# Attention sums on VectorE: two groups taken in turn over the first eight key tiles of a query block

## Chip, cores and metric

The kernel runs on one core of one Trainium2 chip. The metric is the device time of one execution in microseconds (us). Times below come from the runs of the kernel before and from one profiled execution of it.

## What is computed

An attention layer, a residual and layernorm, a linear layer with sign weights, and again residual and layernorm. x is 4 x 2048 x 512 in fp32, with 16 heads of 32:

```
q, k, v = x @ Wq.T, x @ Wk.T, x @ Wv.T            # split into 16 heads of 32
attn    = softmax(q k^T / sqrt(32)) v
x       = layernorm(x + attn)
y       = clip((x @ sign(W).T) * scale + bias, -100, 100)
x       = layernorm(x + y)
```

The change is in the softmax's denominator: the sum over the keys of exp(energy), for each query and head.

## The kernel before, in words

Three stages follow each other: `project` (q, k and v for 16 blocks of 512 tokens), `attend`, and `normalise_and_ffn`. The change lies in `attend`.

`attend` works through 16 items (a batch entry and a group of 4 heads), 4 query blocks of 512 queries each, so 64 query blocks ("blocks" from here, counted from 0). In a block it goes over 16 key tiles of 128 keys. Each tile is two units (two heads each). The engines work like this:

- TensorE (PE), `steps`: in tile step kt it computes the scores of tile kt + 2 (`fast_scores`, L632, transposed: keys on partitions, queries along the free dimension; each unit waits until one of three PSUM slots is free), then the values product of tile kt (`values`, L661), and in tile steps 8 to 14 one of seven pieces of the denominators of the block before (`denominators`, L680), which sums over the partitions by a product with ones. Piece 0 waits for `a_merged`: all three merges of that block. PE takes these in program order.
- ScalarE (ACT), L769: one exponential of 128x1024 for each unit, from PSUM into `probs`, a ring of 8 tiles of 128x2048 fp32. It waits until the slot's old tile has been used by the values product (`a_pv`) and by VectorE (`a_sum`).
- VectorE (DVE), `item`: adds probability tiles. The 16 tiles form four groups. Group 0's sum is made in `total` (two buffers, by the block's parity), groups 1 to 3 in `partial` (one buffer each). Twelve adds a block: the first of a group adds two tiles (L818), and the others add a tile to the sum (L821). Tiles 0 to 3 are group 0, 4 to 7 group 1, 8 to 11 group 2, 12 to 15 group 3, and the adds come at tiles 1, 2, 3, 5, 6, 7, 9, 10, 11, 13, 14, 15. After tile 2's add it copies the block before's output from PSUM (`copy_out`, L797), and after tile 14's add the denominators (`copy_den`, L802). `a_sum` counts the tiles that are summed. An add that uses the sum of the add before waits for `a_sum`.
- GpSimd (POOL), `merge`, L601: for g = 1, 2, 3 it waits until `a_sum` says that the group's last tile is in, issues an accumulating DMA of 1 MB that adds `partial[g - 1]` to `total`, waits until it has landed (`a_merge`) and raises `a_merged`. So merges 1, 2 and 3 of a block run one after the other. In the last block merge 3 is left out, and PE takes both sums instead.
- SyncE (SP) issues the loads of the next item's rows and the stores. Most of the loads of k and v come in an item's fourth block, as tiles are finished; the rows of q come at the blocks' ends.

VectorE's order is written out by hand in `item`; the waits of the other engines are on counts of `a_sum`, `a_prob`, `a_pv`, `a_merged`, `a_den`, `a_out` and `a_dout`. `copy_den` of block b - 1 frees the PSUM bank that the values of block b + 1 write (`a_dout`).

Of the kernel before, what the change touches and what calls it, by code (L numbers as in the profile page):

```python
# [22 lines left out]
ALU = mybir.AluOpType  # L23
# [13 lines left out]
KT = S // P  # L37
# [12 lines left out]
NORM_SQ_MAX = 60000.0 ** 2 / BOUND_SLACK  # L50
GROUPS = 4
PER = KT // GROUPS
P_RING = 8
SLOTS = 3
LAG = 2
# [349 lines left out]
def attend(nc, ctx, dram, banks, ffn, first, early):  # L405
# [5 lines left out]
    def sb(name, shape, dt):  # L411
        return ctx.enter_context(nc.sbuf_tensor(name, shape, dt))

    def sem(name):
        return ctx.enter_context(nc.semaphore(name))
# [4 lines left out]
    k_exact = rows32[0:HD + 1, 1]  # L420
    probs = sb("probs", [P, P_RING, G, BLK], FP32)
    total = sb("total", [P, 2, G, BLK], FP32)
# [17 lines left out]
    a_sum = sem("a_sum")  # L440
# [31 lines left out]
    def out_bank(qb):  # L472

        return 2 * SLOTS + qb % 2
# [4 lines left out]
    def _(sp):  # L479
        def store(it, qb):  # L480

            cols = slice(qb * BLK, (qb + 1) * BLK)
            sp.wait_ge(a_out, it * QB + qb + 1)
            dst = dram["attn"].rearrange("n (g p) t -> (n g) p t", p=P)[bass.ds(it, 1), :, cols]
            sp.dma_start(dst.rearrange("o p t -> (o p) t"), out_sb[:, qb % 2, :]).then_inc(a_store[qb % 2], 16)
            sp.wait_ge(a_dout, it * QB + qb + 1 + 2)
            dst = dram["den"].rearrange("(i h) t -> i h t", h=G)[bass.ds(it, 1), :, cols]
            sp.dma_start(dst.rearrange("o h t -> (o h) t"), den_sb[0:P:HD, qb % 2, :]).then_inc(a_store[qb % 2], 16)
# [11 lines left out]
        with sp.If(needed > 0):  # L500
# [11 lines left out]
            def exact_block(it, n, g, qb, start):  # L512
# [8 lines left out]
                for c in range(QB):  # L521
# [6 lines left out]
                    if qb == 0 and c == 0 and not start:  # L528
                        sp.wait_ge(a_pv, st * KT + P_RING)
                        for vc in range(QB):  # L530
# [17 lines left out]
        with sp.Else():  # L548
# [4 lines left out]
            with sp.Fori(0, LAST) as it:  # L553
# [3 lines left out]
                for qb in range(QB):  # L557
                    st = it * QB + qb
                    if qb == QB - 1:
                        for c in range(QB):  # L560
# [3 lines left out]
                            if c > 0:  # L564
                                sp.wait_ge(a_pv, st * KT + TPB * c + P_RING)
                                load_v(sp, n_ahead, g_ahead, c - 1)
# [4 lines left out]
                    if 0 < qb < QB - 1:  # L571
                        store(it, qb - 1)
                sp.wait_ge(a_pv, (it * QB + QB) * KT + P_RING)
                load_v(sp, n_ahead, g_ahead, QB - 1)
# [8 lines left out]
    def _(pool):  # L583
# [11 lines left out]
        def merge(it, qb, groups):  # L595

            st = it * QB + qb
            for g in groups:
                pool.wait_ge(a_sum, st * KT + PER * (g + 1) + P_RING)
                pool.sem_inc(a_order, 1)  # L600
# [12 lines left out]
    def _(pe):  # L613
        pe.sem_inc(a_pv, P_RING)
        pe.sem_inc(a_den, 2 * len(DEN_TILES))
# [159 lines left out]
    @block.vector  # L775
    def _(dve):
        dve.sem_inc(a_sum, P_RING)
        dve.sem_inc(a_store[0], 32)
        dve.sem_inc(a_store[1], 32)
        needed = dve.value_load(flag[0:1, 0:1])  # L780
        with dve.If(needed > 0):
            dve.wait_ge(a_q[0], FIRST_Q)
            dve.wait_ge(a_k[0], FIRST_K)
            nc.vector.memset(k_exact[HD:HD + 1], 1.0).then_inc(m_ones, 1)
            with dve.Fori(0, N * H) as h:
                for t in range(KT):
                    dve.wait_ge(m_score, h * KT + t + 1)
                    nc.vector.reduce_max(maxima[:, t:t + 1], banks[:, 4 * (t % 2):4 * (t % 2) + 4, :]
                                         .rearrange("p b k -> p (b k)"), AX.X).then_inc(m_max, 1)
                dve.wait_ge(m_T, h + 1)  # L790
                dve.wait_ge(m_store, h * 16 + 16)
                nc.vector.tensor_scalar(max_neg[:], banks[0:KT, 0, 0:P], -1.0, None, ALU.mult).then_inc(m_neg, 1)

        def copy_out(st, parity):
            dve.wait_ge(a_pv, st * KT + KT + P_RING)
            dve.wait_ge(a_store[parity], (st - parity) * 16 + 32)
            nc.vector.tensor_copy(out_sb[:, parity, :], banks[:, out_bank(parity), :]).then_inc(a_out, 1)  # L797

        def copy_den(st, parity):
            dve.wait_ge(a_den, (st + 1 + 2) * len(DEN_TILES))  # L800
            dve.wait_ge(a_store[parity], (st - parity) * 16 + 32)
            nc.vector.tensor_copy(den_sb[:, parity, :], banks[:, out_bank(parity), :]).then_inc(a_dout, 1)  # L802

        def item(it, first):
            for qb in range(QB):
                st = it * QB + qb
                for kt in range(KT):
                    g, place = divmod(kt, PER)
                    if place == 0:
                        continue  # L810
                    into = total[:, qb % 2] if g == 0 else partial[:, g - 1]
                    dve.wait_ge(a_prob, st * UNITS + 2 * kt + 2 + SLOTS)
                    if place == 1:
                        if g == 0:
                            dve.wait_ge(a_den, (st + 1) * len(DEN_TILES))
                        else:
                            dve.wait_ge(a_merged, st * (GROUPS - 1) + g)
                        nc.vector.tensor_tensor(into, probs[:, (kt - 1) % P_RING], probs[:, kt % P_RING], ALU.add).then_inc(a_sum, 2)  # L818
                    else:
                        dve.wait_ge(a_sum, st * KT + kt + P_RING)  # L820
                        nc.vector.tensor_tensor(into, into, probs[:, kt % P_RING], ALU.add).then_inc(a_sum, 1)  # L821
                    if kt == OUT_AFTER and not (first and qb == 0):
                        copy_out(st - 1, (qb - 1) % 2)
                    if kt == DEN_AFTER and not (first and qb == 0):
                        copy_den(st - 1, (qb - 1) % 2)

        for it in range(ITEMS):
            item(it, it == 0)
        copy_out(ITEMS * QB - 1, 1)
        copy_den(ITEMS * QB - 1, 1)  # L830
# [292 lines left out]
class Early:  # L1123
# [26 lines left out]
    def load_v(self, sp, n, g, c):  # L1150
        src = self.v_src[bass.ds(n, 1), bass.ds(g, 1), c].rearrange("o u p t d -> p (o u t) d")
        sp.dma_start(self.v_keys[:, c * TPB:(c + 1) * TPB, :], src).then_inc(self.a_v[c], 16)
# [63 lines left out]
```

## Time and profile before

| what | us |
|---|---|
| runs | 2725.27, 2724.6, 2723.04 |
| median | 2724.6 |
| profiled execution: span from its first to its last instruction | 2721.4 |
| busy in the span: PE, VectorE, ScalarE, GpSimd | 2686.9, 2308.4, 2261.1, 341.1 |
| attention stage, first exponential's start to last one's end | 549.9 to 2427.7 |

The profile gives the profiled execution's span alone; what lies around it isn't shown, and the median of the runs stands 3.2 us above the span. PE's ends are modelled, so its busy time says little about what it could still take. The line numbers are those of the kernel before. A merge's busy time on POOL (0.86 us) is that of issuing it; "to landing" is from its start to the end of its transfer.

### The profile page before, as it was taken

The page shows a single profiled execution, that of the slowest core. Times are in us where ns is not written, and L with a number is a line of the kernel's source. Part 1 is how long each engine was busy: PE and PEld are TensorE (multiplying, and loading weights), DVE is VectorE, ACT ScalarE, POOL GpSimd, SP SyncE. Part 2 cuts the span into 40 slices and gives each one's busy share as a digit, 9 for nine tenths or more (in the row PEclk, how much of TensorE's full clock was granted, in tenths as well). Part 3 has the DMA queues.
Part 4 walks back from the last instruction along what each step waited for, and adds up shares of the span by engine and source line. Part 5 has one row for each costly group of instructions (what it writes and reads, how often), then busy time and mean ns, then how long its engine had stood idle before and what let it go on. Part 6 is the DMA issues. An engine that isn't in the chain of part 4 may idle for free.

```text
span 2721.4 us, 76294 instructions
## 1 busy us (share of the span) xinstructions
PE 2686.9 (99%) x32088; PEld 1351.0 (50%) x32088; DVE 2308.4 (85%) x1983; ACT 2261.1 (83%) x2726; POOL 341.1 (13%) x342
## 2 busy tenths in 40 slices
PE   9999999999999999999999999999999999979998
PEld 8888888733333333333333333333333333337887
DVE  7444444389999999999999999999999999978998
ACT  5333333399999999999999999999999999965665
POOL 1000000000000000010000000000000000005665
PEclk9999999999999999999999999999999999989999
DMA  6555555557686777768677686867768677655553
GB/s 227 191 194 193 188 186 186 197 132 169 132 176 140 155 157 158 162 126 184 138 153 165 142 172 135 167 147 157 168 131 172 141 159 158 150 145 177 189 189 136
DMA packets 216706, 445.22 MB, mean 164 GB/s; under 512 B 15570, under 2 KB 130258, under 8 KB 189780
## 3 DMA queue, kind: packets, MB, share of 16 engines
q0 software_dynamic: 27504, 200.29, 37.4%
q1 hardware_dynamic: 179108, 222.61, 26.2%
q10 hardware_dynamic: 9792, 17.83, 1.7%
q8 instruction: 246, 4.03, 0.6%
q14 instruction: 56, 0.46, 0.1%
HBM read 122.43 MB, written 117.96 MB: 88 GB/s over the span
## 4 chain that ended last, share of the span: by engine, by line
ACT 48%; PE 31%; issue 16%; DMA 3%; DVE 2%; SPq 0%; DVEq 0%; POOL 0%; ACTq 0%; POOLq 0%
ACT probs L769 48%; PE banks L226 19%; PE banks L1007 7%; DMA total<-partial 2%; PE banks L632 1%; PE banks L996 1%; PE banks L661 1%; PE banks L989 1%; PE banks L1003 1%; DVE partial L818 1%; DVE total L821 0%; DVE partial L821 0%; PE banks L248 0%; PE banks L990 0%; PE banks L254 0%
## 5 line engine op out<-in xcount | busy, mean ns | idle before, releaser
L769 ACT ACTIVATE probs<-banks 128x1024 f32<-128x1024 f32 x2048 | 1877.7, 1457 | 3.9 <-PE banks L632 3.9
L632 PE MATMUL banks<-score_rows 97*32 97x512 f16 x16384 | 1117.4, 380 | 4.5 <-issue 4.0
L661 PE MATMUL banks<-probs,v_keys 128*32 128x512 f32 x8192 | 1060.5, 592 | 0.1
L821 DVE TENSOR_TENSOR partial<-partial,probs 128x2048 f32<-128x2048 f32 x384 | 879.4, 2290 | 33.4
L632 PEld LDWEIGHTS banks<-score_rows 97*32 97x32 f16 x16384 | 361.3, 95 | 708.2 <-ACT probs L769 484.3
L818 DVE TENSOR_TENSOR partial<-probs 128x2048 f32<-128x2048 f32 x192 | 439.6, 2290 | 23.6 <-ACT probs L769 16.7
L601 POOL DMA_DIRECT2D total<-partial x191 | 164.7, 862 | 1713.7 <-DMA total<-partial 703.3
L661 PEld LDWEIGHTS banks<-probs,v_keys 128*32 128x32 f32 x8192 | 249.0, 111 | 209.9 <-ACT probs L769 0.2
L821 DVE TENSOR_TENSOR total<-total,probs 128x2048 f32<-128x2048 f32 x128 | 292.6, 2286 | 6.8
L354 DVE TENSOR_TENSOR qk_lo<-banks,qk_hi 128x512 f16<-128x512 f32 x128 | 88.3, 690 | 241.6 <-ACT qk_hi L309 241.6
L680 PEld LDWEIGHTS banks<-total,ones 128*32 128x32 f32 x3584 | 105.6, 109 | 280.7 <-issue 265.1
L309 ACT ACTIVATE qk_hi<-banks 128x512 f16<-128x512 f32 x128 | 76.0, 595 | 184.6 <-PE banks L226 184.6
L226 PE MATMUL banks<-xT_hi,w_hi 128*128 128x512 f32 x512 | 197.3, 389 | 0.0
L226 PE MATMUL banks<-xT_lo,w_hi 128*128 128x512 f32 x512 | 197.2, 389 | 0.0
L226 PE MATMUL banks<-xT_hi,w_lo 128*128 128x512 f32 x512 | 197.2, 389 | 0.0
L818 DVE TENSOR_TENSOR total<-probs 128x2048 f32<-128x2048 f32 x64 | 146.2, 2284 | 7.3 <-ACT probs L769 7.3
L313 ACT ACTIVATE v_out<-banks 128x512 f32<-128x512 f32 x64 | 38.2, 597 | 123.9 <-PE banks L226 123.8
L680 PE MATMUL banks<-total,ones 128*32 128x72 f32 (+1 forms) x3584 | 134.7, 227 | 4.6 <-POOLq L603 4.5
L1021 ACT ACTIVATE std<-mean_var,eps 128x1 f32<-128x1 f32 x128 | 31.8, 289 | 98.0 <-DVE mean_var L1075 97.8
L226 PEld LDWEIGHTS banks<-xT_lo,w_hi 128*128 128x128 f32 x512 | 96.1, 188 | 20.0
L226 PEld LDWEIGHTS banks<-xT_hi,w_lo 128*128 128x128 f32 x512 | 96.1, 188 | 19.9
L226 PEld LDWEIGHTS banks<-xT_hi,w_hi 128*128 128x128 f32 x512 | 96.0, 188 | 19.9
(95 smaller groups left out, 2117.5 us busy)
## 6 DMA issues: line engine op xcount, KB each, us to landing
total<-partial POOLq DMA_DIRECT2D x191, 1024.0 KB, 8.3
scratch_q_raw<-qk_raw SPq DMA_DIRECT2D x16, 1024.0 KB, 5.7
scratch_k_raw<-qk_raw SPq DMA_DIRECT2D x16, 1024.0 KB, 5.7
scratch_v<-v_out SPq DMA_DIRECT2D x16, 1024.0 KB, 5.1
score_rows<-scratch_q_hi SPq DMA_DIRECT2D x128, 128.0 KB, 4.6
score_rows<-scratch_k_hi SPq DMA_DIRECT2D x128, 128.0 KB, 3.5
v_keys<-scratch_v SPq DMA_DIRECT2D x64, 256.0 KB, 5.8
scratch_attn<-wf_scaled SPq DMA_DIRECT2D x64, 256.0 KB
```

The costliest lines, as they stand in the source:

```text
L226: last = nc.tensor.matmul(bank(j), *parts[i], start=(c == 0 and i == 0), stop=(c == DC - 1 and i == 2))
L309: nc.scalar.activation(qk_hi[:, j, :], bank(j), ACT.Copy).then_inc(s_hi, 1)
L313: nc.scalar.activation(v_out[:, j - NQK, :], bank(j), ACT.Copy).then_inc(s_hi, 1)
L354: nc.vector.tensor_tensor(qk_lo[:, j, :], bank(j), qk_hi[:, j, :], ALU.subtract).then_inc(s_lo, 1)
L601: pool.dma_start(total[:, qb % 2], partial[:, g - 1], accum_op=ALU.add).then_inc(a_merge, 16)
L632: last = nc.tensor.matmul(scores_of(phase, unit)[part, i, :], k_rows[:, h, keys], q_rows[:, h, qb * BLK:(qb + 1) * BLK], start=True, stop= ...
L661: last = nc.tensor.matmul(banks[rows, out_bank(qb), :], v_keys[:, kt, rows], probs[:, kt % P_RING, h, :], start=(kt == 0), stop=(kt == KT ...
L680: last = nc.tensor.matmul(banks[rows, out_bank(qb), cols], ones[:], part[:, h, cols], start=(part is parts[0]), stop=(part is parts[-1]))
L769: nc.scalar.activation(probs[:, kt % P_RING, heads, :], scores_of(it % SLOTS, qb * UNITS + u), ACT.Exp, scale=SCALE / GAIN ** 2).then_inc( ...
L818: nc.vector.tensor_tensor(into, probs[:, (kt - 1) % P_RING], probs[:, kt % P_RING], ALU.add).then_inc(a_sum, 2)
L821: nc.vector.tensor_tensor(into, into, probs[:, kt % P_RING], ALU.add).then_inc(a_sum, 1)
L1007: last = nc.tensor.matmul(ffn_bank(s), part[:, s % 4, cols], w[:, c, :], start=False, stop=(c == DC - 1 and w is wf_lo))
```

## The change

VectorE's groups are no longer four consecutive tiles each: over tiles 0 to 7 they alternate, so group 0 has tiles 0, 2, 4 and 6, and group 1 has 1, 3, 5 and 7. Groups 2 and 3 stay 8 to 11 and 12 to 15. The adds come at tiles 2, 3, 4, 5, 6, 7, 9, 10, 11, 13, 14, 15. `PREVIOUS` is the tile of the same group before a tile. `TAKEN` says how many tiles, counted from 0 without a hole, are in a sum after a tile's step; `a_sum` is raised by its steps. An add to a sum waits for the add of its own group's previous tile, which in tiles 4 to 7 isn't the add just before. The merges, their conditions (`a_sum` at 8, 12 and 16 tiles) and everything else stay.

```diff
 GROUPS = 4
 PER = KT // GROUPS
+GROUP_OF = (0, 1) * PER + (2,) * PER + (3,) * PER
+PREVIOUS = tuple(max((e for e in range(kt) if GROUP_OF[e] == GROUP_OF[kt]), default=None) for kt in range(KT))
+
+
+def taken_after(kt):
+
+    used = {e for k in range(kt + 1) if PREVIOUS[k] is not None for e in (PREVIOUS[k], k)}
+    return next(e for e in range(KT + 1) if e not in used)
+
+
+TAKEN = tuple(taken_after(kt) for kt in range(KT))
...
                 for kt in range(KT):
-                    g, place = divmod(kt, PER)
-                    if place == 0:
+                    g, before = GROUP_OF[kt], PREVIOUS[kt]
+                    if before is None:
                         continue
                     into = total[:, qb % 2] if g == 0 else partial[:, g - 1]
                     dve.wait_ge(a_prob, st * UNITS + 2 * kt + 2 + SLOTS)
-                    if place == 1:
+                    if PREVIOUS[before] is None:
                         if g == 0:
                             dve.wait_ge(a_den, (st + 1) * len(DEN_TILES))
                         else:
                             dve.wait_ge(a_merged, st * (GROUPS - 1) + g)
-                        nc.vector.tensor_tensor(into, probs[:, (kt - 1) % P_RING], probs[:, kt % P_RING], ALU.add).then_inc(a_sum, 2)
+                        nc.vector.tensor_tensor(into, probs[:, before % P_RING], probs[:, kt % P_RING],
+                                                ALU.add).then_inc(a_sum, TAKEN[kt] - TAKEN[kt - 1])
                     else:
-                        dve.wait_ge(a_sum, st * KT + kt + P_RING)
-                        nc.vector.tensor_tensor(into, into, probs[:, kt % P_RING], ALU.add).then_inc(a_sum, 1)
+                        dve.wait_ge(a_sum, st * KT + TAKEN[before] + P_RING)
+                        nc.vector.tensor_tensor(into, into, probs[:, kt % P_RING], ALU.add).then_inc(a_sum, TAKEN[kt] - TAKEN[kt - 1])
```

## Rows read from the trace of the kernel before

**Rows 1.** The page: the costliest group of instructions (busy, mean of one, idle)

```profile
L769 ACT ACTIVATE probs<-banks 128x1024 f32<-128x1024 f32 x2048 | 1877.7, 1457 | 3.9 <-PE banks L632 3.9
```

**Rows 2.** Attention stage: busy us of PE, PEld, DVE, ACT, POOL; clock, DMA share, GB/s

```profile
549.90:2427.70 1877.80, 1876.67 (x28088) 688.60 (x28080) 1809.18 (x892) 1877.69 (x2048) 164.72 (x191) 1.00 0.72 152
```

**Rows 3.** The chain of waits in block 3: start, us, what

```profile
654.23 2.30 DVE partial L821
...
657.09 10.06 DMA total<-partial
...
667.87 10.76 DMA total<-partial
...
679.35 7.28 DMA total<-partial
...
686.73 0.34 PE banks L680 x8
```

**Rows 4.** The chain of waits at the end of the attention stage

```profile
2417.23 7.85 DMA total<-partial
...
2425.74 6.98 DMA total<-partial
```

**Rows 5.** VectorE in order of time, blocks 49 (end) and 50: start, us, instruction

```profile
2018.65 2.28 DVE L821 TENSOR_TENSOR partial<-partial,probs 128x2048 f32<-128x2048 f32 x1
2020.85 2.28 DVE L818 TENSOR_TENSOR total<-probs 128x2048 f32<-128x2048 f32 x1
2023.24 2.29 DVE L821 TENSOR_TENSOR total<-total,probs 128x2048 f32<-128x2048 f32 x1
2025.45 0.68 DVE L797 COPY wf_scaled<-banks 128x512 f32<-128x512 f32 x1
2026.05 2.28 DVE L821 TENSOR_TENSOR total<-total,probs 128x2048 f32<-128x2048 f32 x1
2028.25 2.28 DVE L818 TENSOR_TENSOR partial<-probs 128x2048 f32<-128x2048 f32 x1
2030.63 4.69 DVE L821 TENSOR_TENSOR partial<-partial,probs 128x2048 f32<-128x2048 f32 x2
...
2037.84 4.69 DVE L821 TENSOR_TENSOR partial<-partial,probs 128x2048 f32<-128x2048 f32 x2
2042.78 2.29 DVE L818 TENSOR_TENSOR partial<-probs 128x2048 f32<-128x2048 f32 x1 [0.25 <-ACT probs L769]
```

**Rows 6.** Timelines: first exponentials of blocks 50 and 4, PE in block 50

```profile
2016.52 1.43 ACT L769 ACTIVATE probs<-banks 128x1024 f32<-128x1024 f32 x1
667.03 1.43 ACT L769 ACTIVATE probs<-banks 128x1024 f32<-128x1024 f32 x1
2020.31 1.03 PE L661 MATMUL banks<-probs,v_keys 128*32 128x512 f32 x8
2035.80 0.31 PE L680 MATMUL banks<-total,ones 128*32 128x80 f32 x8
```

**Rows 7.** L769 alone, in block 50, then in block 4: duration ns min/median/max

```profile
L769 ACT ACTIVATE probs<-banks x33: 1388/1480/1618, 2015.6 to 2044.9; 128x1024 f32<-128x1024 f32 x33
L769 ACT ACTIVATE probs<-banks x33: 1017/1247/1442, 666.1 to 695.9; 128x1024 f32<-128x1024 f32 x33
```

**Rows 8.** L601's landings, and totals of waits (us, times, longest us)

```profile
DMA to landing us min/median/max: 6.9/8.3/11.1
...
POOL total L601 <- DMA total<-partial: 703.3, 86, 10.3
PEld banks L680 <- POOLq L603: 15.1, 17, 4.9
```

**Rows 9.** Columns of rows 2, block 51, whose first exponential starts at 2045.85

```profile
2045.85:2049.85 4.00, 4.00 (x68) 1.58 (x64) 4.00 (x3) 4.00 (x6) 0.00 (x0) 1.00 0.99 184
2060.00:2063.00 3.00, 3.00 (x48) 1.03 (x44) 2.90 (x2) 3.00 (x5) 0.00 (x0) 1.00 0.61 170
2063.00:2066.00 3.00, 3.00 (x56) 1.08 (x51) 2.88 (x2) 3.00 (x5) 0.77 (x1) 1.00 0.21 60
```

## The prediction

> **What bounds the kernel now.** I read the busy totals first. In the attention stage ScalarE's exponentials (L769) fill 1877.7 us of 1877.8 [rows 1, 2], 0.917 us each, so one query block (32 exponentials) takes 29.33 us and ScalarE has nothing to win: 2048 x 0.9167 is 1877.3, so 0.4 us at most is idle. VectorE is 1809.2 us busy in the same stretch [rows 2] and sits idle until ScalarE delivers (the add of tile 13, 2042.78) [rows 5]. A faster VectorE is therefore worth nothing by itself, and the question is whom VectorE's adds serve, and when.
>
> The chain of waits answers it. Through block 3 of 64 (counted from 0) it leaves ScalarE and runs: VectorE's adds up to tile 7's, then merge 1, merge 2 and merge 3 one after the other, then the first denominator matmul (L680) of the next block [rows 3]. It does so again at the end of the stage: merges 1 and 2 of the last block, released like that, hold the end [rows 4]. POOL issues merge 1 only when the add of tile 7 has ended (654.23 + 2.30 = 656.53, issue at 657.09), and each next merge 0.7 us after the last one landed [rows 3]; a merge takes 6.9 to 11.1 us, median 8.3 [rows 8]. Merge 3 must have landed when PE reaches the denominators in tile step 8 of the next block. I count times within a block from the start of its first exponential: 2016.52 for block 50, 667.03 for block 4. In block 50, undisturbed, the first denominator matmul starts at 2035.80, so at 19.28; in block 4 it starts at 686.73, 19.70, 0.10 after the landing at 686.63, 19.60 [rows 3, 6]. So the deadline for a landing is about 19.15. Behind it there is a cushion: exponentials start before the one ahead has ended. In block 50 they last at least 1.388 us, in block 4 the shortest lasts 1.017 us [rows 7]; 0.38 us of PE's lateness is swallowed that way, and a landing later than 19.53 costs time one for one.
>
> I tabulated all 63 landings of merge 3 (block 3's merge is the one in rows 3) against the first exponential of the block that needs them: 12.4 to 19.6, median 16.8. Block 4's and block 40's (19.60, 19.56) just exceed 19.53; the kernel today loses about 0.1 us to it.
>
> **The change, part by part.** The number of adds stays 12 a block, with the same operands in size, and the counts given to a_sum still sum to 16.
> (a) The first add moves from tile 1 to tile 2. In block 50 tile 13's add started when its tile was ready, at 26.26 [rows 5]; tile 2 is ready 11 x 1.833 earlier, at 6.09. The last add of the block before ends well ahead of that (see c). So the add starts at 6.09, where tile 1's started at 4.33 (2020.85).
> (b) The adds after it. An add that reads the result of the one just before starts 2.40 us after it (2037.84, 2.29 and so on; 2028.25 to 2030.63 is 2.38); one that doesn't starts 2.20 us after (2026.05 to 2028.25) [rows 5]. A copy sits 2.21 us after its add and the next add 0.60 after the copy. Now tiles 2 and 3, 3 and 4, up to 7 alternate: four steps of 2.20. Tile 3 starts at 6.09 + 2.21 + 0.60 = 8.90, tile 7 at 8.90 + 4 x 2.20 = 17.70. Before it was 2030.63 + 2.40 - 2016.52 = 16.51. **Tile 7's add comes 1.2 us later**, although three gaps of 0.19 us are saved: before, it had one more add behind it already.
> (c) The rest: tile 9 at 19.90, 10 at 22.3, 11 at 24.7 (+1.0), 13 at 26.9 (+0.6), 14 at 29.3, the denominator copy at 31.5, tile 15 at 32.1 (+0.6), free again at 34.3, which is 5.0 into the next block. VectorE then waits 1.1 us for tile 2 and the lag doesn't grow.
> (d) What waits for these. Probability slots: tile 0 is released after tile 2's add (8.4) and needed for tile 8, after 14.6; tile 15 after 34.4 - 29.3 = 5.1 and needed after 12.8: no cost. The denominator copy ends near 32.2, 2.9 into the next block; PE's first values there start at 3.79 (2020.31) [rows 6]: 0.9 us of cover is left of 1.6. The partial sum of group 1 is overwritten from 8.9 on, and the merge that reads it has landed by 1 us into the block. No queue gets another DMA; POOL's three waits a block are the same.
> (e) Merges 1, 2, 3. Merge 1 starts 1.2 later; merge 2 and 3 were held by the landing before them (86 of 191 issues by the profile [rows 8]; tile 11's and 15's adds end at 27.0 and 34.4, ahead of the new 29.7 and 39.4). So **merge 3 lands 1.2 us later**. This is the only thing that I price above nothing in the loop.
>
> **The sum.** With 1.2 added, a landing that was later than 18.33 loses. Seventeen are: 19.60, 18.93, 19.05, 18.56, 19.05, 18.62, 18.73, 18.43, 19.39, 18.56, 19.08, 19.27, 19.56, 19.11, 19.44, 19.04, 18.74; the excesses sum to 11.6 us. A replay block by block, with today's merge durations, in which a delay of one block leaves the next that much room, the cushion refills by 0.35 us a block and merge 1 waits for the later of the add and the last merge, gives 10.1. Most of the seventeen are merges of every fourth block (3, 7, 11, ...), in which the next item's rows are loaded: in block 51 the DMA share is 0.61 from 14.2 to 17.2 and 0.21 from there to 20.2, where merge 1 itself (issued at 19.4) has hardly begun [rows 9]. A merge 1 that starts 1.2 later passes the end of this traffic; between none and 0.3 us off these merges I take 0.2, and the replay gives 7.9. At the end merges 1 and 2 of the last block are on the chain [rows 4]: + 1.2. Today's own loss goes off: - 0.1. Together + 9.0 on an execution with a span of 2721.4. The median of the runs stands 3.2 above this span; I carry that over: 2724.6 + 9.0 = 2733.6 us.
>
> The replay is steep. With a shift of 0.4, 0.8, 1.0, 1.2, 1.4 us it gives 1.5, 5.0, 7.4, 10.1, 13.1 us; with every merge 3% longer 25, 3% shorter 1.
>
> **Rivals.**
> 1. The merges give it back (about no change). A merge's duration isn't fixed by its size: 6.9 to 11.1 us [rows 8], and DMA is 0.72 busy in this stage [rows 2]. If a chain that starts 1.2 us later meets less of the loads, its three merges together get shorter. The mechanism decides at 0.5 us off the chain of some 25: what is left of the shift then costs 4.5 us in the loop, with the end's 1.2 just 0.2%. With 0.8 off it is 1.5 + 0.4, so 2726.5. For it: the traffic in rows 9, and the latest landings of today that crowd at 19.0 to 19.1. Against it: merge 2 and 3 run across the start of the next block's loads (share 0.99 there [rows 9]) before and after. 0.22.
> 2. No gap is saved. If an add after an independent one also took 2.40, tile 7's add would start at 8.90 + 4 x 2.40 = 18.50, 2.0 later than today; the replay gives 22.8, the end 2.0: 2749. Against it stand the pairs of tiles 3 and 5 and of 15 and 1, at 2.20 in each block [rows 5]. 0.05.
> The Trainium skill, VectorE: DVE Perf Modes, The DRAIN you can't avoid, says this: every VectorE operation is followed by a pipeline flush, and eight chained copies took the same time with a semaphore after each as with one at the end, "the semaphore costs nothing extra here". By that rule alternating groups saves nothing; this case's trace disagrees, with 2.40 against 2.20 us from start to start.
> 3. Faster. ScalarE's idle 0.4 us is all that the loop could return, less than the 5.4 us (0.2%) that a measurement of this kernel can tell from no change; only a chain at the end that got shorter by several us could do it, and I see none. 0.02.
>
> **Chances and range.** Forecast with the loss as described: 0.71; rivals 0.22, 0.05, 0.02. So faster 0.02, same 0.22, slower 0.76. The range goes down to the case of the merges that give most of it back (2726.5) and up to merges about 1.5% longer than today on the late blocks (2746).
>
> **What would show it.** Tile 7's add starts near 17.7 in a block and the idle time of VectorE moves ahead of tile 2's add; consecutive adds of tiles 3 to 7 stand 2.20 apart. Merge 1 is issued at 20.6 instead of 19.4; merge 3's median landing is near 18.0. PE's waits for POOL at L680 grow from 15.1 us in all [rows 8], the chain of waits runs through the merges in some 15 blocks instead of two or three, and the attention stage grows by some 8 us while the stages before and after it keep their length. I would be wrong if merge 1 started no later, if the landings didn't follow it, or if a late landing had no echo in ScalarE's ends.

## The result: 0.22% slower, and the profile after

The changed kernel takes 2730.61 us (median of 10 runs, 2726.33 to 2734.31), the kernel before 2724.57 us (10 runs, 2722.43 to 2726.13). The ratio is 1.0022, 95% interval 1.0013 to 1.0031: 6.0 us, with the interval reaching from 3.5 to 8.4. The forecast was 2733.6 in a range of 2726.5 to 2746. Medians and ratios, here and below, leave out four executions in the slow state, of 4600 to 15800 us (three of the kernel before, one of the late start alone).

The profiled execution took 2733.11 us, with a span of 2731.3. It is one of the slower ones of its kernel, so the differences of the two profiles (9.9 us of span) overstate the median's. A second profile of each kernel is among the experiments below.

The attention stage, in the columns of rows 2 (PE, PEld, DVE, ACT, POOL, clock, DMA share, GB/s), answers to [rows 2]:

```profile
550.30:2438.60 1888.30, 1875.72 (x28091) 697.12 (x28080) 1786.66 (x892) 1880.06 (x2048) 164.57 (x191) 1.00 0.71 151
```

It lasts 1888.3 us where it lasted 1877.8: 10.5 longer, and this is where all the time went. VectorE is busy for 22 us less, though its work is the same: neighbouring adds that don't wait for each other overlap by 0.08 us, the view counts that once, and there are four more such pairs in a block (4 x 0.08 x 64 = 20 us, an estimate that leaves 2 us of the 22 unexplained). Fewer busy microseconds on an engine didn't make a faster kernel.

VectorE in block 50, whose first exponential starts at 2025.98, answers to [rows 5] (start, us, instruction, idle before it):

```profile
2028.65 2.28 DVE L833 TENSOR_TENSOR partial<-partial,probs 128x2048 f32<-128x2048 f32 x1
2031.98 2.29 DVE L829 TENSOR_TENSOR total<-probs 128x2048 f32<-128x2048 f32 x1 [1.04 <-ACT probs L780]
2034.18 0.68 DVE L808 COPY wf_scaled<-banks 128x512 f32<-128x512 f32 x1
2034.79 2.28 DVE L829 TENSOR_TENSOR partial<-probs 128x2048 f32<-128x2048 f32 x1
2036.98 2.28 DVE L833 TENSOR_TENSOR total<-total,probs 128x2048 f32<-128x2048 f32 x1
2039.19 2.28 DVE L833 TENSOR_TENSOR partial<-partial,probs 128x2048 f32<-128x2048 f32 x1
2041.39 2.28 DVE L833 TENSOR_TENSOR total<-total,probs 128x2048 f32<-128x2048 f32 x1
2043.59 2.28 DVE L833 TENSOR_TENSOR partial<-partial,probs 128x2048 f32<-128x2048 f32 x1
```

The idle 1.04 us ahead of tile 2's add is new. From tile 3 on the adds stand 2.20 apart. Tile 7's add starts at 2043.59, which is 17.61 in this block (median of the blocks 17.66), where it was 16.51. POOL issues merge 1 at 2046.54, 20.56 in the block; the median over the blocks is 20.52 after 19.39.

The chain of waits through block 39 into block 40, whose first exponential starts at 1730.41 (start, us, what):

```profile
1721.56 9.23 DMA total<-partial
...
1731.51 10.78 DMA total<-partial
...
1743.01 9.11 DMA total<-partial
...
1752.21 0.35 PE banks L691 x8
```

Merge 3 lands at 1752.12, 21.71 in the block. PE in order of time at that place:

```profile
1748.80 1.03 PE L672 MATMUL banks<-probs,v_keys 128*32 128x512 f32 x8
1752.21 0.35 PE L691 MATMUL banks<-total,ones 128*32 128x80 f32 x8 [2.38 <-POOLq L614]
1752.37 1.05 PE L643 MATMUL banks<-score_rows 97*32 97x512 f16 x16
```

PE stands for 2.38 us ahead of the first denominator piece, and the scores queued behind it come that much later. ScalarE's exponentials after it show that no cushion is left, since their shortest is what an exponential takes with nothing queued (duration ns, min/median/max, to compare with [rows 7]):

```profile
L780 ACT ACTIVATE probs<-banks x4: 1014/1020/1027, 1753.0 to 1755.8; 128x1024 f32<-128x1024 f32 x4
```

The waits in all (us, times, longest), to compare with 15.1 us in [rows 8]:

```profile
PEld banks L691 <- POOLq L614: 34.7, 24, 5.1
...
PE banks L691 <- POOLq L614: 16.7, 14, 4.2
...
ACT probs L780 <- PE banks L643: 12.1, 12, 4.3
```

The last row is ScalarE idle. In the kernel before it was idle once, 3.9 us, at the stage's start. Here the 4.3 us are that start, and eleven idle times inside the stage are new, 7.9 us together. In the page's shares of the chain that ended last, the merges ("DMA total<-partial") hold 13% of the span, where they held 2%.

### The profile page after: what moved, and what is told of

It is laid out like the page before. It is cut to its first block, busy times and chain, and to the rows that moved or that the text cites. A ratio compares the mean times of both kernels' runs of the same rounds, so it can differ in the third digit from the quotient of the medians.

```text
span 2731.3 us, 76294 instructions
## 1 busy us (share of the span) xinstructions
PE 2684.6 (98%) x32088; PEld 1358.4 (50%) x32088; DVE 2286.5 (84%) x1983; ACT 2263.3 (83%) x2726; POOL 340.9 (12%) x342
## 4 chain that ended last, share of the span: by engine, by line
ACT 31%; PE 21%; DMA 13%; issue 12%; DVE 1%; POOLq 0%; POOL 0%; SPq 0%; DVEq 0%; ACTq 0%
ACT probs L780 31%; DMA total<-partial 13%; PE banks L1019 6%; PE banks L643 6%; PE banks L672 6%; PE banks L1008 1%; PE banks L1001 1%; DVE partial L833 1%; PE banks L691 1%; PE banks L1015 1%; DVE partial L829 0%; PE banks L1002 0%; ACT y L1037 0%; DMA den_in<-scratch_den 0%; DVE stats L1082 0%
## 5 line engine op out<-in xcount | busy, mean ns | idle before, releaser
L780 ACT ACTIVATE probs<-banks 128x1024 f32<-128x1024 f32 x2048 | 1880.1, 1394 | 12.4 <-PE banks L643 12.1
L643 PEld LDWEIGHTS banks<-score_rows 97*32 97x32 f16 x16384 | 367.8, 95 | 700.1 <-ACT probs L780 469.4
L237 PEld LDWEIGHTS banks<-xT_hi,w_lo 128*128 128x128 f32 x512 | 96.1, 188 | 19.9
```

The lines of the kernel that those rows point to most:

```text
L237: last = nc.tensor.matmul(bank(j), *parts[i], start=(c == 0 and i == 0), stop=(c == DC - 1 and i == 2))
L643: last = nc.tensor.matmul(scores_of(phase, unit)[part, i, :], k_rows[:, h, keys], q_rows[:, h, qb * BLK:(qb + 1) * BLK], start=True, stop= ...
L780: nc.scalar.activation(probs[:, kt % P_RING, heads, :], scores_of(it % SLOTS, qb * UNITS + u), ACT.Exp, scale=SCALE / GAIN ** 2).then_inc( ...
```

## The experiments

Two numbers stand for each profile, both tabulated block by block as the prediction did for the kernel before: the **excess**, the sum of what merge 3's landings exceed 19.53 us by, and the **loss**, the sum of what the blocks from 1 on last beyond 29.33 us, from the end of one block's last exponential to the next (with 29.33 taken as 32 x 0.9167 = 29.333). The theory was that merge 1 starts later, merge 3 therefore lands later, and what is late beyond the cushion is lost. The rivals were that VectorE's own later adds and its later denominator copy cost the time, that the alternation itself does, or that the runs differ for another reason.

**A later merge with VectorE untouched.** In the kernel before, a clear of 128x1100 on GpSimd between merge 1's wait and its issue:

```diff
             for g in groups:
                 pool.wait_ge(a_sum, st * KT + PER * (g + 1) + P_RING)
+                if g == 1:
+                    pool.wait_ge(m_spin, st + 1)
+                    pool.sem_inc(a_order, 1)
+                    nc.gpsimd.memset(spin[:], 0.0).then_inc(m_spin, 1)
+                    pool.wait_ge(m_spin, st + 2)
```

(The lines that make `spin` and its semaphore are left out, here and in the next run.)

> The kernel before with one clear of 128x1100 on GpSimd put between merge 1's wait for VectorE and merge 1's issue in every block; VectorE's order is untouched. Theory (the cost of the change is merge 1 starting late, so that merge 3 misses TensorE's first denominator piece): merge 1 is issued about 1.1 to 1.3 us later (estimate from the 0.53 us of a 128x512 clear on GpSimd), merge 3's landings move as much, some 13 to 15 blocks lose time, + 5 to + 12 us against the kernel before. Rival (the cost comes through VectorE's own later adds and later denominator copy): no change, within 2 us, since VectorE does nothing later.

Measured: 2733.74 us (5 runs) against 2723.91 (27 runs), ratio 1.0036 (1.0023 to 1.005), + 9.8 us. The clear takes 1.02 us; merge 1 is issued at 20.58 (median), the waits at the denominators grow as in the changed kernel:

```profile
PEld banks L688 <- POOLq L611: 37.1, 29, 5.3
PE banks L688 <- POOLq L611: 15.4, 14, 4.4
ACT probs L777 <- PE banks L640: 11.5, 9, 4.3
```

and the stage lasts 1886.8 us with VectorE's adds where they were (tile 7's at 16.51):

```profile
550.00:2436.80 1886.80, 1875.52 (x28088) 696.83 (x28080) 1809.44 (x892) 1879.52 (x2048) 229.55 (x255) 1.00 0.71 151
```

So a merge that starts 1.2 us later is enough for the whole cost. The rival of VectorE's later adds isn't needed. By the medians this run is even 3 us slower than the changed kernel, though its excess and loss lie between those of the changed kernel's two profiles (the table below). Its last stage is 1.2 us longer, with more of it at the lower clock (the last section), and the rest isn't explained; the two intervals, 6.3 to 13.6 us and 3.5 to 8.4, overlap.

**The same clear where it should be hidden**, ahead of merge 1's wait:

```diff
             for g in groups:
+                if g == 1:
+                    pool.wait_ge(m_spin, st + 1)
+                    pool.sem_inc(a_order, 1)
+                    nc.gpsimd.memset(spin[:], 0.0).then_inc(m_spin, 1)
+                    pool.wait_ge(m_spin, st + 2)
+                    pool.sem_inc(a_order, 1)
                 pool.wait_ge(a_sum, st * KT + PER * (g + 1) + P_RING)
```

> The same clear, but ahead of merge 1's wait for VectorE, where GpSimd is idle. Theory: no change, within 2 us of the kernel before, landings as before. A rival for the run with the clear behind the wait (the clear itself disturbs VectorE or the transfers): as slow as that run.

Measured: 2726.54 us (11 runs), ratio 1.0011 (1.0002 to 1.002), + 2.6 us: more than expected, and the step that I had overlooked is visible. The clear is hidden only while POOL is idle there. Where merge 3 of the block before lands late, the clear starts after it: after landings at 19.16 and 19.32 merge 1 is issued at 21.54 and 21.69 instead of 19.4 to 20.5. In most blocks merge 1 goes at 19.40 as before. The excess is 3.5 us, the loss 3.5, in four blocks. It is a weak dose of the same mechanism, not a free control; it does show that the clear by itself does no harm in the other 60 blocks. That the loss again equals the excess, to 0.1 us, speaks for the chain too, since here the clear moved only some of the merges.

**The deadline moved.** The denominators in six pieces from tile step 9 on, in the changed kernel and in the kernel before:

```diff
-DEN_TILES = tuple(range(8, 15))
-DEN_EDGES = (0, 80, 152, 224, 296, 368, 440, BLK)
+DEN_TILES = tuple(range(9, 15))
+DEN_EDGES = (0, 88, 172, 256, 340, 424, BLK)
```

> The changed kernel with the denominators in six pieces at tile steps 9 to 14 instead of seven at 8 to 14, so that TensorE wants merge 3's landing 1.85 us later. VectorE's adds are as in the changed kernel. Theory: no landing of merge 3 is late any more; the loss in the attention stage goes to below 1 us, the time returns to within 2 us of the kernel before. Rival (VectorE's later adds of tiles 13 to 15 and its later denominator copy cost the time): it stays 4 to 8 us slower than before.

> The kernel before with the same six pieces at tile steps 9 to 14. Theory: few of its landings are late, so at most 1 us is gained, and the difference between this run and the changed kernel with six pieces is within 1.5 us: that is what the change costs when the deadline is moved. Should the larger pieces cost TensorE time by themselves, both six-piece kernels show it.

Measured: the changed kernel with it 2724.49 us (11 runs), ratio to the kernel before 1.0002 (0.9993 to 1.0011); the kernel before with it 2722.41 (11 runs), ratio 0.9994 (0.9985 to 1.0003), 1.5 us less where at most 1 was expected, and not told from no change. The stage of the changed kernel with it, in which VectorE is as late as without it (tile 7's add at 17.58, tile 15's at 31.98):

```profile
550.20:2428.00 1877.80, 1877.80 (x27588) 678.72 (x27577) 1785.52 (x892) 1877.54 (x2048) 164.51 (x191) 1.00 0.71 152
```

Four of its landings are still later than 19.53 (excess 3.1), and the loss is 0.02: lateness costs nothing once TensorE asks for the sum a tile later. Between the two six-piece kernels 2.1 us are left, a little more than the 1.5 expected. Of these 0.2 is the stage; the last merge of the stage lands 5.60 us after the last exponential in the one and 4.21 in the other, which is the cost at the stage's end (+ 1.4). Some of the 2.1 may be TensorE's clock: the mean granted clock over the whole execution was 0.992 in eight of the eleven runs of the one and in one of the eleven of the other, and the last section shows that such runs are the longer ones.

**The late start alone.** The kernel before with its groups and gaps; only tile 1's add waits for tile 2:

```diff
-                    dve.wait_ge(a_prob, st * UNITS + 2 * kt + 2 + SLOTS)
+                    late = 1 if kt == 1 else 0
+                    dve.wait_ge(a_prob, st * UNITS + 2 * (kt + late) + 2 + SLOTS)
```

> The kernel before, its groups and all its gaps kept, with the first add of a block waiting for tile 2 instead of tile 1: the late start of the change alone. Theory: tile 7's add starts at 6.09 + 2.40 + 2.21 + 0.60 + 2.20 + 2.40 + 2.40 = 18.3, 1.8 us later than before and 0.6 later than in the changed kernel; the replay gives about 19 us in the loop: + 12 to + 22 us against the kernel before, clearly slower than the changed kernel. Rival (the alternation costs the time, the late start doesn't): within 2 us of the kernel before.

Measured: 2735.66 us (5 runs) against 2723.73 (21 runs), ratio 1.0044 (1.0031 to 1.0057), + 11.9 us. Tile 7's add starts at 18.26, merge 1 goes at 21.16. It lies just under what was expected: the replay's 19 us was too much, the profile has a loss of 12.5, with 16 landings beyond 19.53. So of the two halves of the change the late start costs 12 us, and the alternation gives 6 of them back.

**The same with the deadline moved**, the edit of the six pieces on top:

> The late first add of the kernel with all gaps kept (it was 12.2 us slower than before), with the six denominator pieces at tile steps 9 to 14. Its landings of merge 3 are the latest of all. Theory: at most one or two blocks still lose time; the loss in the loop falls from 12.5 us to under 1.5, the time to + 1 to + 3.5 us against the kernel before, with 1.2 of it at the stage's end. Rival (VectorE's own lateness costs): it stays more than 8 us slower.

Measured: 2724.95 us (11 runs), ratio 1.0004 (0.9995 to 1.0013). Fourteen landings lie beyond 19.53 (excess 8.7) and the loss is 0.02. What was 11.9 us is 0.9, just under the 1 to 3.5 that were expected.

**The alternation without the late start.** In the changed kernel's code:

```diff
-GROUP_OF = (0, 1) * PER + (2,) * PER + (3,) * PER
+GROUP_OF = (0, 0, 0, 0, 1, 1, 0, 1) + (2,) * PER + (3,) * PER
```

> Groups of tiles 0, 1, 2, 3, 6 and of 4, 5, 7: the adds come at tiles 1, 2, 3, 5, 6, 7 as in the kernel before, and the adds of tiles 5, 6 and 7 alternate. So two gaps go without the late start. Theory: tile 7's add starts 0.4 us earlier than before, merge 3 lands 0.4 earlier; - 1 to + 0.5 us against the kernel before, since little was lost there. Rival (alternating groups is itself what costs): slower than before by over 2 us.

Measured: 2722.86 us (11 runs), ratio 0.9995 (0.9986 to 1.0004), - 0.9 us and not told from no change. Tile 7's add starts at 16.14 (0.38 earlier), merge 1 at 19.01. The adds of tiles 5, 6 and 7 stand 2.20 apart. Alternating costs nothing.

**And with the copy of the output behind tile 7's add** (`OUT_AFTER = 7` on top of it):

> The same groups, and the copy of the output moved from behind tile 2's add to behind tile 7's: merge 1's wait ends 0.8 us earlier than in the kernel before, the copy ends at about 18.2 in the block, ahead of the 19.15 at which TensorE's first denominator piece wants it. Theory: - 2 to 0 us against the kernel before, of which up to 0.8 at the end of the stage. Should the copy come too late for TensorE, it shows as waits for VectorE at the denominators.

Measured: 2724.18 us (11 runs), ratio 1.0002 (0.9993 to 1.0011). Merge 1 goes at 18.88, only 0.13 earlier than without it and 0.51 earlier than in the kernel before, where 0.8 was expected: with the copy gone, tile 3's add needs the 2.40 again and tile 5's waits for its tile. No landing is late, so there was nothing left to win.

**The two edits for the better together**, tiles 5 to 7 alternating after an early start, and the six pieces:

> The groups 0, 1, 2, 3, 6 and 4, 5, 7 together with the six denominator pieces at tile steps 9 to 14: merge 1 starts 0.4 us earlier than before and the deadline is 1.85 us later. Theory: the attention stage is at the pace of the exponentials (1877.3 to 1877.8 us) in every execution, merges at the stage's end come 0.4 us earlier; - 2.5 to - 0.5 us against the kernel before, and a narrower spread upwards. Rival (the kernel before loses nothing by its landings): no change.

Measured: 2723.71 us (11 runs) against 2724.03, ratio 0.9998 (0.9989 to 1.0007): no gain that can be told from none, where 0.5 to 2.5 us were expected. No landing is later than 18.9, and the runs reach from 2721.66 to 2724.24. The stage took 1878.8 us, outside the 1877.3 to 1877.8 that were expected for every execution: its blocks from 1 on lose nothing, but block 0, ahead of which there is no merge, took 30.75 us, after 29.62 in the kernel before. None of these versions is measurably faster than the kernel before, which fits a stage that already runs at the pace of its exponentials.

**Second profiles of both kernels.**

> The changed kernel once more, for a second profile. Theory: the spread of its runs (2726.3 to 2734.3) is that of merge 3's landings: the loss in the attention stage differs from the first profile's 10.0 us by about as much as the whole time does, and equals the sum of what its landings exceed 19.53 by. Rival: the stage is as long as in the first profile and the difference lies in the other stages.

> The kernel before once more, for a second profile. Theory: its landings of merge 3 lie on the near side of 19.53 in all but a few blocks again, the attention stage lasts 1877.5 to 1880 us.

Measured: 2730.8 us and 2723.73 us, spans 2729.0 and 2721.9. The stages, changed kernel first:

```profile
550.00:2436.50 1886.50, 1874.85 (x28093) 696.93 (x28082) 1786.88 (x892) 1879.30 (x2048) 164.48 (x191) 1.00 0.71 151
```
```profile
549.80:2427.50 1877.70, 1877.17 (x28092) 690.53 (x28080) 1809.68 (x892) 1877.58 (x2048) 164.49 (x191) 1.00 0.72 152
```

The changed kernel's span is 2.3 us shorter than in its first profile, 1.8 of it in the stage (loss 8.0 after 10.0). The theory of the spread is that the merges' durations differ between executions and a late landing is now paid for, while in the kernel before most of that variation falls short of the deadline. These two profiles fit it, and so does the changed kernel with the deadline moved: its eleven runs lie within 2.2 us, where the ten without that spread over 8.

All profiles together, in us:

| kernel | tile 7's add | merge 1 issued | excess | loss |
|---|---|---|---|---|
| before, two profiles | 16.52, 16.52 | 19.39, 19.43 | 0.1, 0.2 | 0.2, 0.2 |
| changed, two profiles | 17.66, 17.66 | 20.52, 20.52 | 10.2, 7.9 | 10.0, 8.0 |
| before, clear behind the wait | 16.51 | 20.58 | 8.7 | 8.6 |
| before, clear ahead of the wait | 16.53 | 19.40 | 3.5 | 3.5 |
| before, late start | 18.26 | 21.16 | 12.1 | 12.5 |
| before's start, tiles 5 to 7 alternating | 16.14 | 19.01 | 0.1 | 0.0 |
| the same, copy of the output behind tile 7 | 16.01 | 18.88 | 0.0 | 0.0 |
| before, six pieces | 16.46 | 19.34 | 0.0 | 0.0 |
| changed, six pieces | 17.58 | 20.44 | 3.1 | 0.0 |
| late start, six pieces | 18.22 | 21.09 | 8.7 | 0.0 |
| tiles 5 to 7 alternating, six pieces | 16.08 | 18.95 | 0.0 | 0.0 |

In every kernel of the table with the deadline at step 8 the loss equals the excess within 0.4 us. The two are read from different places, the landings of the transfers and the ends of the exponentials, and that is the theory's strongest support. The times in the second and third column are medians over the blocks.

## Why the prediction was right, point by point

- **What bounds the kernel**: as said. The exponentials' pace sets the stage wherever no landing is late (1877.4 to 1878.0 us, and 1878.8 once, through block 0), and the saved gaps on VectorE gain nothing there. The edge of 19.53 was rounded: the rows give 19.28 - 0.10 + 0.37 = 19.55, a difference that changes none of the readings.
- **(a), (b), (c), VectorE's times**: tile 2's add at 6.05 (forecast 6.09), tile 7's at 17.66 (17.70), tile 15's at 32.05 (32.1). The saved gap is 0.19 us, four in a row at 2.20. Rival 2, that nothing is saved, is out.
- **(d), what was priced at nothing**: the runs with the deadline moved leave VectorE as late as in the changed kernel, and the stage loses nothing; no other wait took over.
- **(e), the merges**: merge 1 starts 1.13 us later (forecast 1.2). Merge 3's median landing moved less, from 16.8 to 17.4, where 18.0 was forecast: the shift shrank in the three easy blocks of four and stayed nearly whole in the fourth (from 18.9 to 20.0 in the mean, in the second pair of profiles from 19.0 to 19.9), and those are the ones that count.
- **The size of the loss**: 7.9 us forecast in the loop, 10.0 and 8.0 in the two profiles. One term had the wrong reason: I took 0.2 us off merge 1 in every fourth block for the loads that it would miss, and there it took 9.3 us in the mean after 8.9, in both pairs of profiles, while merge 3 took 0.3 to 0.4 less. The three merges of those blocks together changed by + 0.1 us in the first pair and - 0.1 in the second, so the term was nearly nothing. Without it the replay said 10.1. It said 19 for the late start, which lost 12.5, so its agreement at 1.2 us is partly luck: it holds the merges' durations fixed, and they aren't.
- **The cost at the stage's end** was put at 1.2 us and wasn't paid in the profiles: the last landing came 5.21 and 5.23 us after the last exponential, after 5.03 and 5.38 before, because the last block's merge 1 was shorter (6.9 us in both, before 7.9 and 8.1). In the six-piece pair it was 1.4. The term is real on average at most, and hidden in the merges' spread.
- **The last stage** was assumed unchanged. It was 1.3 to 1.8 us shorter, see below. This and the point above come to some 3 us, as much as 2733.6 was too high; the sizes are those of two profiles, so that the sum fits is in part chance.
- **Rival 1**, that the merges give it back, had 0.22. It holds in part: the chains of three blocks in four did get shorter (their three merges by 0.2 us in the mean), and the late ones didn't by more than 0.1.

## What to carry to other kernels

On an engine that isn't the bound, count not how busy it is but when its result for someone else is ready: follow the chain from there to the engine that is, find the deadline and the cushion, and tabulate the slack over all rounds, since the mean slack (here over 2 us) says nothing about the few rounds that pay. A reordering that removes gaps but starts later moves the result by the late start less the gaps, and both have to be worked out up to the result that someone waits for. Where durations vary between executions, moving the deadline by one step can do more than shaving the chain: here it took back 5.4 of 6.0 us and 11.0 of 11.9, by the differences to the kernel before. In the kernel before, where almost nothing was late, it gained nothing that could be measured.

## What the runs showed of the hardware

An add on VectorE that waits for the one just before starts 2.40 us after it, one that waits for the one before that 2.20, shorter than the 2.28 that each lasts: neighbours overlap by 0.08 us if nothing ties them.

ScalarE's exponentials start before the one ahead has ended and last 1.01 us with nothing queued and up to 1.64 with a queue, while their ends stand 0.917 apart in both cases. The duration of one is therefore a measure of how far ahead the feeding engine is, and its least value, 1.01, marks the point where lateness becomes loss.

The last stage, from its first reciprocal to the end, took 277.4 and 276.9 us in the two profiles of the kernel before and 275.6 twice in the changed one, with the same code. TensorE's granted clock was at the lower of its two levels (1.2 of 2.4 GHz) for different stretches at that stage's start, after the idle time at the end of attention. The 35 us that begin 12.3 and 12.4 us after the last exponential, in the kernel before and in the changed one (columns of rows 2):

```profile
2440.00:2475.00 35.00, 26.14 (x122) 21.62 (x123) 21.55 (x62) 13.37 (x25) 14.56 (x13) 0.70 0.50 176
```
```profile
2451.00:2486.00 35.00, 24.86 (x128) 20.80 (x129) 22.61 (x64) 13.78 (x25) 15.49 (x16) 0.77 0.52 186
```

The mean granted clock is 0.70 and 0.77, and the first group of twelve linear-layer products in the chain of waits takes 4.10 us in the one and 2.81 in the other:

```profile
2458.46 4.10 PE banks L1007 x12
```
```profile
2469.72 2.81 PE banks L1019 x12
```

Over all thirteen profiles the last stage's length follows the mean granted clock in the 35 us behind the last exponential:

| mean granted clock there | last stage, us | profiles |
|---|---|---|
| 0.71 | 275.6 to 275.7 | changed (two), late start with seven and with six pieces, copy of the output behind tile 7 |
| 0.66 | 276.8, 276.9 | before (second), clear behind the wait |
| 0.61 | 277.4, 277.4 | before (first), tiles 5 to 7 alternating with six pieces |
| 0.56 | 277.3 to 277.7 | clear ahead of the wait, six pieces in the changed kernel and in the one before, tiles 5 to 7 alternating |

So some 2 us of a run's time are decided there, in kernels whose last stage is the same code. The runs without a profile show it too: of the kernel before, the 20 executions with a mean granted clock of 0.992 took 2725.1 us in the mean and the 20 with 0.995 took 2722.8. A difference of 2 us between two versions is therefore not the versions' own unless it is found in their stages. What decides the clock's course at the stage's start stays open.

Left open too: why the merges of block 39 land so late (in the changed kernel's two profiles theirs is the latest landing of all, in the kernel before's the second and the twelfth of 63), and why the time for one 1 MB merge reaches from 6.9 to 11.5 us over all profiles. The loads may explain a part, which no run tested: the merges of every fourth block, with the most traffic beside them, are the slowest in the mean (merge 2: 9.9 to 10.0 us in the profiles of the two kernels, in the others 7.7 to 9.1).
